# Attention half-steps reordered, and the change from experts to channel attention made half by half

## The chip, the cores and the metric

The kernel runs on one core of a Trainium2 chip. The metric is the device time of one execution in microseconds; lower is better. TensorE (PE) multiplies matrices and turns tiles, VectorE (DVE), ScalarE (ACT) and GpSimd (POOL) work on rows and elements, SyncE (SP) issues the transfers. Each has a queue of its own that runs in the order in which it was written, and they meet at semaphores.

## The reference

1,024 rows of 256 values (16 batches of 64 rows) go through four stages, each added to x behind a gain.

```
x = x + tanh(g_xattn[0]) * gated_attention(layernorm(x), ctx)    # 16 heads in 8 groups, own and cross, inputs rounded to fp8
x = x + tanh(g_ffn[0])   * experts(layernorm(x))                 # 32 experts, 8 chosen: silu(x wg) * (x wu) * share, then wd
x = x + tanh(g_xattn[1]) * channel_attention(layernorm(x), ctx)  # softmax over channels within each batch, 8 heads
x = x + tanh(g_ffn[1])   * mlp(layernorm(x))                     # four-bit weights: gelu(gate) * up, then down
```

## The kernel before, in words

**Gated attention** works in 16 units, two for each group: the first 512 rows, then the rest. Unit h has four tiles of 128 rows. Step h of the pipeline does the projections and norms of unit h, the scores and softmax of unit h-1 and the outputs of unit h-2. The order within a step is written by hand, once for each engine, in its `step(h)`. For tile i: TensorE's `project` puts queries, keys and values in PSUM; ScalarE's `squares` sums squares and `copy_values` takes the values; GpSimd's `rstd_of` makes the reciprocal deviation (an addition and a power); VectorE's `normalise` scales the rows; TensorE's `turn_tile` turns them; ScalarE's `keys` and VectorE's `queries` take the result. For half r of a unit: `scores`, VectorE's `shift` (maximum and difference), ScalarE's `exponent`, VectorE's `totals`, GpSimd's `normalise_probs`, TensorE's `turn_probs`, ScalarE's `probs_out`, TensorE's `values`, ScalarE's `take`, VectorE's `quantise` (five operations of rounding to fp8), TensorE's `outputs`, VectorE's `add_outputs`. `values(u, 0)` also waits for `add_outputs` of unit u-1.

The weights of the next group are prepared meanwhile. Even steps run `sum_weights` and `centre_weights` on w_in (halves c) and ScalarE's `weights_high`; odd steps run `weights_low` and `output_weights_low` (wp_lo). w_in and wp_in have one buffer each. SyncE issues w_in(g) once `weights_low` of group g-1 is done, then wp_in(g) once `output_weights_low` of group g-1 is done; so w_in(g+1) stands in the queue behind wp_in(g).

**Experts and the last stage** share `gated_mlp`: steps j and b, blocks of 128 hidden units, halves of 512 rows. A half block does two products (gate, up), then the previous one's `down` adds into four PSUM banks. At the end ScalarE copies these to outT, TensorE turns them into eight tiles, VectorE adds them to x in four updates. **Channel attention** then makes statistics, scaled rows h and their high and low parts (split); TensorE's `replicate` spreads them, `row_scores` go to VectorE's `maxima`, four pairs of heads a batch, and after `take_maxima` the loop over 16 batches begins. Ahead of the first product stand eight filler matmuls (`keep_busy`).

## Time and profile before

| what | us |
|---|---|
| median of 3 runs | 942.41 |
| lowest, highest | 941.45, 947.39 |
| the profiled execution's own time | 944.11 |
| its span in the trace | 942.30 |
| PE, DVE, ACT, POOL busy | 839.4, 707.2, 542.3, 320.5 |

The profiled execution is 1.8 us longer than its span, which leaves out what lies around the instructions, and 1.7 us above the median. Busy shares are means over stages with different limits. A line of a timeline has start and duration in us, engine, source line, operation, and what it writes and reads; a bracket tells how long the engine was idle before it and what ended that.

### The profile page before, as it was taken

The numbers are of one execution on the slowest core, as the hardware profiler recorded it, in microseconds if no ns is written. First come the engines' busy times: TensorE is split into PE (matmuls) and PEld (weight loads), VectorE is DVE, ScalarE is ACT, GpSimd is POOL, SyncE is SP. The second block draws the span as 40 slices with busy tenths as digits, with TensorE's granted clock in tenths as the row PEclk, the third lists the DMA queues.
The fourth block names the chain that finished last, engine by engine and source line by source line (L and its number), as shares of the span: only waits on it lengthen the run. The fifth ranks groups of instructions, "written<-read, shape, count | busy, mean of one in ns | idle before, by whom it ended". The sixth has DMA issues, their size and how long they took to land. (4 is left out here: it accounts for less than half of the span.)

```text
span 942.3 us, 16846 instructions
## 1 busy us (share of the span) xinstructions
PE 839.4 (89%) x6150; PEld 673.3 (71%) x6152; DVE 707.2 (75%) x1071; ACT 542.3 (58%) x1579; POOL 320.5 (34%) x458
## 2 busy tenths in 40 slices
PE   1678989998999899976999999998999997999997
PEld 1567788777877887864777888886555554888886
DVE  7787989999998998788575555555898986466643
ACT  5667778787877787752543333332577774333432
POOL 1233444444443444333333222210333544042420
PEclk9878999999999999979999999999999997999999
DMA  4101010101010100005323333220100002101001
GB/s 160 45 2 67 1 69 2 68 2 69 1 68 1 68 2 24 1 2 211 101 73 115 108 113 105 96 64 31 40 1 2 2 2 67 34 34 54 14 0 45
DMA packets 13705, 46.26 MB, mean 49 GB/s; under 512 B 1952, under 2 KB 5376, under 8 KB 11328
## 3 DMA queue, kind: packets, MB, share of 16 engines
q1 hardware_dynamic: 13488, 45.27, 14.0%
q8 instruction: 43, 0.70, 0.3%
q14 instruction: 30, 0.25, 0.1%
q10 hardware_dynamic: 144, 0.03, 0.0%
HBM read 44.12 MB, written 1.18 MB: 48 GB/s over the span
## 5 line engine op out<-in xcount | busy, mean ns | idle before, releaser
L418 ACT ACTIVATE square<-ps 128x128 bf16<-128x128 f32 x384 | 100.6, 287 | 31.6 <-PE ps L242 31.4
L242 PE MATMUL ps<-wt_hi,xq 128*128 128x512 f32 (+1 forms) x256 | 90.8, 371 | 11.4 <-DVE wt_lo L650 10.7
L1333 POOL TENSOR_TENSOR moe_w_lo<-moe_w_all,moe_w_hi 128x384 fp32r<-128x384 f32 x48 | 56.3, 1206 | 121.9 <-ACT moe_w_hi L1436 121.9
L575 POOL TENSOR_TENSOR rstd<-rstd,half_neg 128x6 f32<-128x6 f32 x64 | 94.5, 1476 | 5.0
L242 PE MATMUL ps<-wt_lo,xq 128*128 128x512 f32 (+1 forms) x256 | 85.7, 355 | 0.0
L580 POOL TENSOR_TENSOR probs<-probs,total 128x512 f32<-128x512 f32 x32 | 45.7, 1428 | 117.5 <-DVE total L696 117.5
L1788 ACT ACTIVATE ca_probs<-ps 128x512 f32<-128x512 f32 x128 | 69.5, 594 | 26.9 <-PE ps L1704 26.0
L1452 ACT CAST moe_in_hi<-moe_inner 128x512 fp32r<-128x512 f32 x48 | 29.8, 621 | 93.7 <-DVE moe_inner L1516 93.7
L418 ACT ACTIVATION_READ_ACCUMULATOR square<-ps 128x1 f32 x384 | 83.5, 218 | 0.0
L668 DVE TENSOR_TENSOR qn<-ps,rstd 128x768 f32<-128x768 f32 x64 | 60.4, 952 | 30.6 <-POOL rstd L575 30.4
L1370 PE MATMUL ps<-moe_hT_hi,moe_w_hi 128*128 128x512 f32 x192 | 75.7, 394 | 5.0 <-POOL moe_w_lo L1333 4.4
L1873 DVE TENSOR_REDUCE context_mx<-ps 128x4 f32<-128x1024 f32 x64 | 75.9, 1210 | 3.5 <-PE ps L1678 3.3
L251 PE MATMUL ps<-ident,qn 128*128 128x128 f32 x256 | 43.2, 294 | 38.1 <-DVE qn L668 37.7
L1370 PE MATMUL ps<-moe_hT_hi,moe_w_lo 128*128 128x512 f32 x192 | 75.4, 393 | 0.0
L1370 PE MATMUL ps<-moe_hT_lo,moe_w_hi 128*128 128x512 f32 x192 | 75.3, 392 | 0.0
L1506 DVE TENSOR_TENSOR moe_act_g<-moe_act_g,ps 128x512 f32<-128x512 f32 x48 | 33.0, 687 | 53.5 <-PE ps L1370 53.5
L242 PEld LDWEIGHTS ps<-wt_hi,xq 128*128 128x128 f32 x256 | 52.0, 203 | 20.7 <-DVE wt_lo L650 11.1
L1333 POOL TENSOR_TENSOR ffn_w_lo<-ffn_w_all,ffn_w_hi 128x384 fp32r<-128x384 f32 x28 | 34.5, 1263 | 84.8 <-ACT ffn_w_hi L1436 84.8
L571 POOL TENSOR_TENSOR rstd<-sumsq,eps 128x6 f32<-128x6 f32 x64 | 21.1, 330 | 119.3 <-ACT square L418 119.3
L251 PEld LDWEIGHTS ps<-ident,qn 128*128 128x128 f32 x256 | 28.7, 145 | 44.9 <-DVE qn L668 43.5
L315 PE MATMUL ps<-wp_hi,catq 128*128 128x256 f32 x240 | 59.3, 287 | 0.3 <-DVE catq L101 0.3
L315 PE MATMUL ps<-wp_lo,catq 128*128 128x256 f32 x240 | 58.9, 285 | 0.0
(229 smaller groups left out, 2432.5 us busy)
## 6 DMA issues: line engine op xcount, KB each, us to landing
moe_w_all<-in_experts SPq DMA_DIRECT2D x8, 1152.0 KB, 6.2
w_in<-in_wt SPq DMA_DIRECT2D x8, 1024.0 KB, 5.8
moe_shares<-route_rows SPq DMA_DIRECT2D x14, 384.0 KB, 3.7
wp_in<-in_wp SPq DMA_DIRECT2D x8, 512.0 KB, 3.5
moe_shares<-route_rows SPq DMA_DIRECT2D x14, 256.0 KB, 3.8
ffn_codes<-in_codes SPq DMA_DIRECT2D x8, 384.0 KB, 3.4
ffn_w_scales<-in_code_scales SPq DMA_DIRECT2D x8, 384.0 KB, 4.0
moe_shares<-route_rows SPq DMA_DIRECT2D x14, 128.0 KB, 3.1
```

Of the source, the lines that this page charges most:

```text
L242: last = mm(ps[:, first + bank, col:col + width], left[:, c, tokens], w[:, c, wcol:wcol + width], start=(j == 0), stop=(j == len(steps) - 1))
L251: last = nc.tensor.transpose(ps[:, bank, j * P:j * P + P], qn[:, i % 2, j, :], ident[:])
L315: last = mm(ps[:, out_bank(u) + j, q * HID:q * HID + HID], catq[:, f // HPG, f % HPG, t * P:t * P + P], w[:, f, :], start=(n == 0), stop=( ...
L418: last = nc.scalar.activation(square[:, i % 2, j, :], ps[:, bank, (j % 4) * P:(j % 4) * P + P], ACT.Square, scale=float(HD) ** -0.5, accum ...
L575: nc.gpsimd.tensor_tensor(rstd[:, i % 2, :], rstd[:, i % 2, :], k.half_neg[:, 0:6], ALU.pow).then_inc(s["rstd_ready"], 1)
L580: nc.gpsimd.tensor_tensor(probs[:, r], probs[:, r], total[:, r, :].unsqueeze(2).broadcast_to([P, 8, SEQ]), ALU.mult).then_inc(s["probs_rea ...
L668: nc.vector.tensor_tensor(qn[:, i % 2], both[:, 0:6], rstd[:, i % 2].unsqueeze(2).broadcast_to([P, 6, HD]), ALU.mult).then_inc(s["normed"], 1)
L1333: last = nc.gpsimd.tensor_tensor(w_lo[:, b, cols], w_all[:, b, cols], w_hi[:, b, cols].bitcast(F32), ALU.subtract)
L1370: last = mm(ps[:, bank, :], w[:, b, col:col + P], h[:, c, tokens], start=(n == 0), stop=(n == len(steps) - 1))
L1506: nc.vector.tensor_tensor(act_g[:, half, :], act_g[:, half, :], ps[:, U_BANK, :], ALU.mult).then_inc(s["gated"], 1)
L1788: nc.scalar.activation(probs[:, head, :], ps[:, B_BANK + n % 3, :], ACT.Exp, scale=float(C_DIM) ** -0.5).then_inc(s["b_taken"], 1)
L1873: nc.vector.tensor_reduce(dst, ps[:, bank:bank + 2, :].rearrange("p e (q l) -> p e q l", q=CH), AX.X, ALU.max).then_inc(s["a_taken"], 1)
```

## The change

In attention TensorE does the first projection, turns the probabilities of unit h-2, and does the value products ahead of turning tile 0; the value products of (h-1, 0) go ahead of turning tile 3. ScalarE follows that order. VectorE sums both halves of the next group's weights at the start of even steps, centres them ahead of the second shift, makes half of weights_low at the start of odd steps, and does the totals of (h-1, 1) ahead of the additions. In `gated_mlp` the last step's blocks run all of the first half, then all of the second; the first half is turned and added to x under the last blocks. From experts to channel attention the first half's statistics and rows are made there too; the second half is turned, added and scaled within channel attention, where the filler matmuls are gone. Changes of names, slots and counters that follow from that are left out; so is `turned_bank`, which puts the first half in banks 2 and 3.

```diff
@@ -349,15 +349,16 @@
                 here = is_unit(h)
                 if here:
                     project(h, 0)
-                    project(h, 1)
                 if is_unit(h - 2):
                     turn_probs(h - 2, 1)
+                if here:
+                    project(h, 1)
                 if is_unit(h - 1):
                     scores(h - 1, 0)
+                if is_unit(h - 2):
+                    values(h - 2, 1)
                 if here:
                     turn_tile(h, 0)
-                if is_unit(h - 2):
-                    values(h - 2, 1)
                 if is_unit(h - 1):
                     scores(h - 1, 1)
                 if here:
@@ -370,9 +371,10 @@
                     turn_probs(h - 1, 0)
                 if here:
                     turn_tile(h, 2)
-                    turn_tile(h, 3)
                 if is_unit(h - 1):
                     values(h - 1, 0)
+                if here:
+                    turn_tile(h, 3)
             pe.wait_ge(s["ident_in"], 16)
             for q in range(4):
@@ -466,21 +468,22 @@
                 g, here = h // 2, is_unit(h)
                 if here:
                     squares(h, 0)
-                    copy_values(h, 0)
-                    squares(h, 1)
                 if is_unit(h - 2):
                     probs_out(h - 2, 1)
                 if here:
+                    copy_values(h, 0)
+                    squares(h, 1)
                     copy_values(h, 1)
+                if is_unit(h - 2):
+                    take(h - 2, 1)
+                if here:
                     keys(h, 0)
                 if is_unit(h - 1):
                     exponent(h - 1, 0)
-                if is_unit(h - 2):
-                    take(h - 2, 1)
+                if here:
+                    keys(h, 1)
                 if h % 2 == 1 and g + 1 < GROUPS:
                     weights_high(g + 1, 1)
-                if here:
-                    keys(h, 1)
                 if h == 0:
                     scale_rows(3)
@@ -488,27 +491,28 @@
                     squares(h, 2)
                     copy_values(h, 2)
                     squares(h, 3)
+                if is_unit(h - 1):
+                    exponent(h - 1, 1)
+                if h % 2 == 0 and h > 0 and g + 1 < GROUPS:
+                    weights_high(g + 1, 0)
+                if here:
                     copy_values(h, 3)
                 if is_unit(h - 1):
-                    exponent(h - 1, 1)
+                    probs_out(h - 1, 0)
                 if h % 2 == 1 and g < GROUPS:
                     output_weights_high(g)
-                if h % 2 == 0 and h > 0 and g + 1 < GROUPS:
-                    weights_high(g + 1, 0)
-                if is_unit(h - 1):
-                    probs_out(h - 1, 0)
                 if here:
                     keys(h, 2)
+                if is_unit(h - 1):
+                    take(h - 1, 0)
+                if here:
                     keys(h, 3)
                 if h == 0:
                     weights_high(1, 0)
-                if h == 0:
                     act.wait_ge(s["c_in"], 16)
                     for c in range(CH):
                         nc.scalar.copy(ctx_hi[:, c, :], ctx_in[:, c, :]).then_inc(s["c_high"], 1)
-                if is_unit(h - 1):
-                    take(h - 1, 0)
             act.dma_start(vec[:], a["vec"]).then_inc(s["v_in"], 16)
@@ -754,6 +758,11 @@
             def step(h):
                 g, here = h // 2, is_unit(h)
                 ahead = g + 1 < GROUPS
+                if ahead and h % 2 == 0 and h > 0:
+                    sum_weights(g + 1, 0)
+                    sum_weights(g + 1, 1)
+                if ahead and h % 2 == 1:
+                    weights_low(g + 1, 0)
                 if here:
                     normalise(h, 0)
                 if is_unit(h - 1):
@@ -766,31 +775,30 @@
                 if h == 0:
                     quantise_rows(2)
+                    sum_weights(1, 0)
                 if is_unit(h - 2):
                     quantise(h - 2, 1)
                 if ahead and h % 2 == 0:
-                    sum_weights(g + 1, 0)
+                    centre_weights(g + 1, 0)
+                if ahead and h % 2 == 0 and h > 0:
+                    centre_weights(g + 1, 1)
                 if ahead and h % 2 == 1:
-                    weights_low(g + 1, 0)
                     weights_low(g + 1, 1)
                 if is_unit(h - 1):
                     shift(h - 1, 1)
-                if ahead and h % 2 == 0:
-                    centre_weights(g + 1, 0)
                 if here:
                     normalise(h, 2)
-                    normalise(h, 3)
+                if is_unit(h - 1) and h < LAST:
+                    totals(h - 1, 1)
                 if is_unit(h - 2):
                     add_outputs(h - 2, 0)
                     add_outputs(h - 2, 1)
                 if here:
+                    normalise(h, 3)
                     queries(h, 2)
-                if ahead and h % 2 == 0:
-                    sum_weights(g + 1, 1)
-                if is_unit(h - 1) and h < LAST:
-                    totals(h - 1, 1)
-                if ahead and h % 2 == 0:
-                    centre_weights(g + 1, 1)
+                if h == 0:
+                    sum_weights(1, 1)
+                    centre_weights(1, 1)
                 if h % 2 == 1 and h < LAST:
                     output_weights_low(g)
                 if h == 0:
...
+        HALF = TILES // 2
+        def blocks(j, b):
+            if isinstance(j, int) and (j, b) == (STEPS // 2 - 1, 1):
+                return [(blk, half) for half in range(2) for blk in range(NBLK)]
+            return [(blk, half) for blk in range(NBLK) for half in range(2)]
+        def at(j, b, p):
+            return 2 * NBLK * (2 * j + b) + p
+        def turns_first_half(j, b, p):
+            return isinstance(j, int) and (j, b, p) == (STEPS // 2 - 1, 1, NBLK + 1)
...
+        def share_slot(j, n):
+            return 2 if isinstance(j, int) and (j, n) == (STEPS // 2 - 1, 2 * NBLK - 1) else n % 2
...
             with pool.Fori(1, STEPS // 2) as j:
                 low(j, 0, True)
                 low(j, 1, True)
+            if moe:
+                k.channel.gpsimd_rstd(pool, 0)
...
+            def turn_out(half):
+                for o in range(CH):
+                    pe.wait_ge(s["out_copied"], CH * half + o + 1)
+                    for t in range(HALF * half, HALF * half + HALF):
+                        last = nc.tensor.transpose(ps[:, turned_bank(t // 2), (t % 2) * HID + o * P:(t % 2) * HID + o * P + P],
+                                                   outT[:, o, t * P:t * P + P], ident[:])
+                        if o == CH - 1 and t % 2:
+                            last.then_inc(s["turned"], 1)
...
+                    for p in range(2 * NBLK):
+                        half_block(j, b, p, first=first and (b, p) == (0, 0))
+                        if turns_first_half(j, b, p):
+                            turn_out(0)
+                        if p > 0:
+                            down(j, b, p - 1)
+                        elif b > 0:
+                            down(j, 0, 2 * NBLK - 1)
+                        elif not first:
+                            down(j - 1, 1, 2 * NBLK - 1)
             pe.wait_ge(turn.low, 2 * CH)
             if moe:
                 router.tensor_logits(pe)
             steps(0, True)
-            with pe.Fori(1, STEPS // 2) as j:
+            with pe.Fori(1, STEPS // 2 - 1) as j:
                 steps(j, False)
...
+            steps(STEPS // 2 - 1, False)
+            down(STEPS // 2 - 1, 1, 2 * NBLK - 1)
+            if not moe:
+                turn_out(1)
...
+            def out_copy(half):
+                act.wait_ge(s["d_done"], at(STEPS // 2 - 1, 1, NBLK * (half + 1)))
+                for o in range(CH):
+                    nc.scalar.copy(outT[:, o, half * 512:half * 512 + 512], ps[:, OUT + 2 * o + half, :]).then_inc(s["out_copied"], 1)
...
+                            if turns_first_half(j, b, n - 2 * NBLK * b):
+                                out_copy(0)
...
+            inner_high(STEPS // 2 - 1, 1, 2 * NBLK - 1, False)
+            if moe:
+                k.channel.scalar_high(act, 0)
+            out_copy(1)
         @block.vector
+            def update_rows(q):
+                dve.wait_ge(s["turned"], q + 1)
+                rows = x[:, 2 * q:2 * q + 2, :].rearrange("p t o -> p (t o)")
+                nc.vector.scalar_tensor_tensor(rows, ps[:, turned_bank(q), :], k.gain[:, gain:gain + 1], rows, ALU.mult, ALU.add
+                                               ).then_inc(s["x_updated"], 1)
...
+                if turns_first_half(j, b, p):
+                    update_rows(0)
+                if moe and last_step and p == NBLK + 2:
+                    k.channel.vector_means(dve)
                 dve.wait_ge(s["in_hi_done"], v + 1)
...
+                if turns_first_half(j, b, p):
+                    update_rows(1)
+                    if moe:
+                        k.channel.vector_stats(dve)
...
+            if moe:
+                k.channel.vector_rows(dve)
+            else:
+                for q in range(HALF // 2, TILES // 2):
+                    update_rows(q)
...
+    def vector_stats(self, dve):
+        for n in range(self.HALF):
+            dve.wait_ge(self.ends["x_updated"], n // 2 + 1)
+            self.nc.vector.bn_stats(self.stats[:, n, :], self.k.x[:, n, :]).then_inc(self.s["stats_done"], 1)
...
+    def vector_rows(self, dve):
+        row_scale(self.nc, dve, self.k.x, self.h, self.mv, self.rstd, self.s["rstd_step"], 0, self.s["row_normed"], (0,))
+        self.vector_low(dve, 0)
+    def scalar_high(self, act, t):
+        act.wait_ge(self.s["row_normed"], t + 1)
+        split_high(self.nc.scalar.copy, self.split, self.h, t, t + 1, self.s["h_high"])
...
+    def tensor_last(self, pe, banks):
+        for q, bank in enumerate(banks):
+            for o in range(CH):
+                pe.wait_ge(self.ends["out_copied"], CH + o + 1)
+                for t in range(2):
+                    tile = self.HALF + 2 * q + t
+                    last = self.nc.tensor.transpose(self.k.ps[:, bank, t * HID + o * P:t * HID + o * P + P],
+                                                    self.outT[:, o, tile * P:tile * P + P], self.k.ident[:])
+            last.then_inc(self.ends["turned"], 1)
+    def vector_last_update(self, dve, banks):
+        for q, bank in enumerate(banks):
+            dve.wait_ge(self.ends["turned"], self.HALF // 2 + q + 1)
+            rows = self.k.x[:, self.HALF + 2 * q:self.HALF + 2 * q + 2, :].rearrange("p t o -> p (t o)")
+            self.nc.vector.scalar_tensor_tensor(rows, self.k.ps[:, bank, :], self.k.gain[:, 2:3], rows, ALU.mult, ALU.add
+                                                ).then_inc(self.ends["x_updated"], 1)
...
+        LAST_BANKS = (OUT_BANK, B_BANK + 2)
...
-            keep_busy(nc, k, OUT_BANK, 8)
             pe.wait_ge(s["h_low"], 2)
             replicate(0, 0)
             replicate(0, 1)
+            k.channel.tensor_last(pe, LAST_BANKS)
             row_scores(0, 0)
+            pe.wait_ge(k.channel.ends["x_updated"], TILES // 2)
             replicate(1, 0)
             row_scores(0, 1)
             replicate(1, 1)
...
-            for t in range(FIRST_TILES):
-                act.wait_ge(s["row_normed"], t + 1)
-                split_high(nc.scalar.copy, split, h, t, t + 1, s["h_high"])
             for b in range(2):
                 for group in range(2):
                     take_rows(b, group)
+                    if (b, group) == (0, 0):
+                        for t in range(1, FIRST_TILES):
+                            k.channel.scalar_high(act, t)
...
                 pool.wait_ge(s["weighed"], i + 1)
-            row_rstd(nc, pool, mv, rstd, k.half_neg, s["stats_done"], 0, s["rstd_step"], 0)
+            def rest_high(first, last, n0):
+                pool.wait_ge(s["row_normed"], last)
+                for par in range(2):
+                    pool.wait_ge(*((s["values_set"], 2) if n0 + par == 0 else (s["rest_high"], n0 + par)))
+                    dst = split[0:64].rearrange("p (n b) f -> p n b f", b=2)[:, first:last, par]
+                    nc.gpsimd.tensor_copy(dst, h[64 * par:64 * par + 64, first:last]).then_inc(s["rest_high"], 1)
             pool.wait_ge(k.context.values_scaled, 1)
             values(0)
             values(1)
...
-            pool.wait_ge(s["rest_high"], 2)
+            k.channel.gpsimd_rstd(pool, 1)
+            rest_high(FIRST_TILES, TILES // 2, 0)
+            rest_high(TILES // 2, TILES, 2)
+            pool.wait_ge(s["rest_high"], 4)
             for b in range(2, BATCH):
                 values(b)
                 if b > 2 and b % 2 == 0:
...
-            row_stats(nc, dve, x, stats, mv, s["stats_done"], 0)
-            row_scale(nc, dve, x, h, mv, rstd, s["rstd_step"], 0, s["row_normed"])
-            for t in range(FIRST_TILES):
-                dve.wait_ge(s["h_high"], 2 * t + 2)
-                split_low(nc, split, h, t, t + 1, s["h_low"])
-            for pair in range(PAIRS):
-                maxima(0, pair)
+            k.channel.vector_last_update(dve, LAST_BANKS)
+            maxima(0, 0)
+            k.channel.vector_last_stats(dve)
+            maxima(0, 1)
+            for t in range(1, FIRST_TILES):
+                k.channel.vector_low(dve, t)
+            maxima(0, 2)
+            k.channel.vector_last_rows(dve)
+            maxima(0, 3)
             take_maxima(0)
             maxima(1, 0)
             for b in range(BATCH):
```

## Rows read from the trace of the kernel before

**Rows 1.** PE, PEld, DVE, ACT, POOL, clock, DMA of each pair of steps

```profile
76.40:126.63 50.23, 46.95 (x418) 39.97 (x417) 43.16 (x63) 38.17 (x152) 20.07 (x21) 0.97 0.09 33
126.63:173.07 46.44, 41.86 (x417) 37.61 (x416) 42.55 (x61) 35.86 (x146) 20.30 (x21) 0.96 0.09 35
173.07:221.16 48.09, 43.82 (x404) 37.47 (x403) 43.61 (x63) 36.68 (x148) 21.14 (x21) 1.00 0.09 34
221.16:266.61 45.45, 40.60 (x417) 36.27 (x416) 43.07 (x61) 36.09 (x146) 20.53 (x21) 1.00 0.10 36
266.61:315.45 48.84, 44.87 (x403) 38.78 (x403) 43.00 (x63) 36.55 (x148) 21.02 (x21) 0.97 0.09 34
315.45:360.91 45.46, 40.58 (x416) 36.27 (x416) 43.09 (x61) 36.08 (x146) 20.57 (x21) 1.00 0.10 36
```

**Rows 2.** Timeline of DVE at the start of an even step

```profile
219.96 1.17 DVE L656 TENSOR_TENSOR wp_lo<-wp_in,wp_hi 128x1024 fp32r<-128x1024 f32 x1
...
224.01 1.23 DVE L101 TENSOR_TENSOR catq<-scaled,power 128x1024 fp32r<-128x1024 bf16 x1
226.45 0.96 DVE L668 TENSOR_TENSOR qn<-ps,rstd 128x768 f32<-128x768 f32 x1 [1.21 <-POOL rstd L575]
```

**Rows 3.** Timeline of SP, the issue of w_in in that step

```profile
221.53 0.43 SPq L195 DMA_DIRECT2D w_in<-in_wt  x1
```

**Rows 4.** The tile w_in: its eight transfers, from issue to landing

```profile
DMA to landing us min/median/max: 5.0/5.8/6.9
```

**Rows 5.** Timeline of PE there: turning tile 0, then value products

```profile
227.46 0.66 PE L251 MATMUL ps<-ident,qn 128*128 128x128 f32 x4 [2.17 <-DVE qn L668]
...
228.26 1.16 PE L301 MATMUL ps<-pT,v_rows 64*128 64x128 f32 x16
```

**Rows 6.** Timeline of DVE, the rest of that step

```profile
231.12 0.43 DVE L97 TENSOR_SCALAR scaled<-scaled 128x1024 bf16<-128x1024 bf16 x1
...
235.09 0.94 DVE L633 TENSOR_REDUCE w_mean<-w_in 128x6 f32<-128x768 f32 x1
...
239.88 1.27 DVE L720 TENSOR_TENSOR acc<-acc,ps 128x512 f32<-128x512 f32 x2
...
244.30 1.27 DVE L97 TENSOR_SCALAR scaled<-scaled 128x1024 bf16<-128x1024 bf16 x1
...
248.43 0.96 DVE L668 TENSOR_TENSOR qn<-ps,rstd 128x768 f32<-128x768 f32 x1
```

**Rows 7.** Timeline of ACT, the take of (h-1, 0)

```profile
242.52 1.57 ACT L451 ACTIVATE scaled<-ps,r_smooth 128x256 bf16<-128x256 f32 x4 [0.18 <-PE ps L301]
```

**Rows 8.** Timeline of POOL, the probabilities of (h-1, 1)

```profile
243.64 1.65 POOL L580 TENSOR_TENSOR probs<-probs,total 128x512 f32<-128x512 f32 x1 [5.21 <-DVE total L696]
```

**Rows 9.** Groups of DVE by shape, 130 to 361 us: first quantising operation

```profile
L97 DVE TENSOR_SCALAR scaled<-scaled 128x1024 bf16<-128x1024 bf16 x19 | 14.1, 742 | 3.5 <-ACT scaled L451 3.5
```

**Rows 10.** Timeline of PE in step 14, its wait

```profile
367.48 0.65 PE L251 MATMUL ps<-ident,qn 128*128 128x128 f32 x4 [1.55 <-DVE qn L668]
```

**Rows 11.** Timeline of DVE in step 1, its wait

```profile
46.56 0.96 DVE L668 TENSOR_TENSOR qn<-ps,rstd 128x768 f32<-128x768 f32 x1 [2.00 <-POOL rstd L575]
```

**Rows 12.** Windows, columns as in rows 1 (the clock third from last)

```profile
135.00:140.00 5.00, 5.00 (x58) 4.54 (x57) 3.93 (x9) 2.80 (x6) 1.04 (x1) 0.79 0.00 0
...
652.70:665.40 12.70, 10.26 (x42) 5.42 (x40) 10.43 (x32) 3.77 (x8) 6.52 (x21) 1.00 0.35 125
...
785.00:790.00 5.00, 1.93 (x16) 0.58 (x16) 3.91 (x15) 2.43 (x3) 0.00 (x0) 0.56 0.00 0
```

**Rows 13.** Timeline of DVE from experts to channel attention

```profile
653.48 2.73 DVE L1554 SCALAR_TENSOR_TENSOR x_rows<-ps,gain,x_rows 128x512 f32<-128x512 f32 x4 [2.42 <-PE ps L1419]
...
665.44 4.62 DVE L1873 TENSOR_REDUCE context_mx<-ps 128x4 f32<-128x1024 f32 x4 [0.83 <-PE ps L1678]
...
671.02 1.23 DVE L1873 TENSOR_REDUCE context_mx<-ps 128x4 f32<-128x1024 f32 x1
```

**Rows 14.** Timeline of DVE at the end of the kernel

```profile
936.67 2.72 DVE L1554 SCALAR_TENSOR_TENSOR x_rows<-ps,gain,x_rows 128x512 f32<-128x512 f32 x4 [2.40 <-PE ps L1419]
```

142 lines of the change are left out of this document (70 added, 72 removed).

## The prediction

> **What bounds the kernel now.** I first read the split of the span into stages, one line for each pair of attention steps [rows 1]. Read the time of a pair beside its VectorE time. T stands here for the end of wp_lo, the low part of the output weights, which closes each pair of VectorE's queue. In the five pairs from 126.63 to 360.91 VectorE is busy 42.55 to 43.61 us of 45.45 to 48.84, TensorE 40.58 to 44.87. Neither is full: VectorE's idle time is 234.28 - 215.32 = 18.96 us in the five pairs, 3.8 us a pair. That is the most this reordering can win there.
>
> Then the order of time on VectorE. Behind T comes the quantising of (h-1, 0), to 225.24, and a wait of 1.21 us for the reciprocal deviation that GpSimd makes of ScalarE's squares; normalise(h, 0) starts at 226.45, T + 5.3 us [rows 2]. TensorE waits 2.17 us for that result, turns it, and only then does value products (1.16 us) [rows 5]. So both edits aim at real holes. At the change from experts to channel attention VectorE's four updates of x start at 653.48, the four maxima of the first batch at 665.44 and the next batch's first, from which on the loop runs, at 671.02 [rows 13]: there a serial chain bounds the time.
>
> **The sums half a step early.** In even steps sum_weights(g+1, 0) and (g+1, 1) now stand ahead of normalise(h, 0). They read w_in, which has one buffer. SyncE's queue has not changed: it issues w_in only behind wp_in, which waits for the same wp_lo. The issue is at 221.53, T + 0.4 [rows 3], and landing takes 5.8 us (5.0 to 6.9) [rows 4]: the weights are there at T + 6.2. VectorE would be free at 225.24, T + 4.1. Before, the first sum ran at 235.09, 14 us after T, and the transfer was hidden; now VectorE waits 2.1 us, makes both sums, 0.94 us each less overlap (1.75 us) [rows 6], and normalise(h, 0) starts near T + 7.9 instead of T + 5.3. Queued behind it are shift(h-1, 0), normalise(h, 1) and the quantising; TensorE's turn_tile(h, 0) waits for it, and ScalarE's keys for that. The 1.2 us wait for GpSimd disappears beneath the new wait.
>
> **Odd steps.** Half of weights_low (1.45 us, half of a block of about 3) goes to the head of the step, where it fills the wait for GpSimd. Some odd steps have such a wait, the one at 248.43 has none [rows 6]. This half of the edit costs nothing by itself.
>
> **Later in the step.** Before, the outputs' additions end at 241.1 [rows 6] and the take of (h-1, 0) at 244.1 [rows 7]: additions, value products, ScalarE's take form a chain of 3.0 us to the next quantising. VectorE covered it with a queries copy, a sum, totals and a centring; at 244.30 it starts without a wait. In the changed order the sum, the totals and the centring stand earlier, and only normalise(h, 3) and queries remain, 0.87 + 0.72 = 1.6 us. These two are the pitches of their rows, and the difference is a new wait of VectorE, 1.4 us in even steps. In odd steps wp_lo (1.17) [rows 2] still covers it but for 0.3. Totals earlier do help in another place: GpSimd's multiplication of probs, 1.65 us from 243.64 [rows 8], collides with the first quantising operation, which takes 1.27 us at 244.30 [rows 6]. The same operation has a mean of 742 ns over 19 calls, and a free one takes 0.43 [rows 6], so the excess is 0.31 x 19 = 6.0 us in five pairs [rows 9]. I credit 0.84 us a pair, that of the even step; behind the odd one stands the wait for w_in, which eats it.
> The Trainium skill, page Advanced Engine Details and Errata, section Mode Summary, says that VectorE's second port is shared with GpSimd, so that two-port operations and GpSimd's block each other. By that rule the quantising that no longer meets GpSimd is a free one each time. The trace agrees, with 1.27 us where GpSimd runs.
>
> **Value products ahead of transposes.** values(h-2, 1) moves into the hole before turn_tile(h, 0) at 1.1 us a step. In even steps that hole grows by more than 1.1, and scores(h-1, 1) waits for shift(h-1, 0), which is behind normalise anyway; so there it wins nothing. It wins where no weights are prepared: steps 14 and 15 where TensorE's wait is 1.55 us in step 14 [rows 10], and I take 1.1 off each, together -2.2 us. values(h-1, 0) ahead of turn_tile(h, 3) lets ScalarE take earlier: ScalarE then still owes keys(h, 3) before squares(h+1, 0), which leaves VectorE an odd-step wait of about 0.7 us.
>
> **Sum of attention.** A pair is VectorE's work, 43.06 - 0.84 = 42.2, plus idle 2.1 + 0.3 + 1.4 + 0.7, plus the small gaps that it has now, what is left of its 3.8 us of idle time without the marked waits, an estimate of 1.0 us: 47.7 with rounding. Five pairs 238.5 against 234.28: +4.2 us; the light pairs (45.45) lose 2.2 us each and the heavy ones (48.09, 48.84) win about 1 or less. The pair of 50.23 us (76.40 to 126.63) is long today, with VectorE idle for 7.1; with 47.7 and half a microsecond for its clock it is -1.8 or so. In step 1 weights_low fills a wait of 2.00 us at 46.56 [rows 11]: -1.3. **Clock:** between 135 and 140 us the granted clock is 0.79 [rows 12], so TensorE ran part of it at 1.2 GHz, behind a wait of an even step like that at 227.46. Two of the five pairs show a clock under 1.00 [rows 1]. The light pair with such a drop takes 46.44 and one without 45.45: 0.9 us for a drop. TensorE's wait before turn_tile is now about 3.1 us in each even step, so I expect four drops, +3.4 us (bounds: 0, and six at twice the price, 11). Attention: 4.2 - 1.8 - 1.3 - 2.2 + 3.4 = +2.3 us.
>
> **Experts to channel attention.** Half of the updates, stats, scalings and the first low split go into or behind the last expert blocks, where VectorE has waits. The eight early transposes cost TensorE some 0.9 us there, on the path, so its last product ends near 653.7 and the second half's first update, behind ScalarE's copy, the end of the block, the replicas and transposes, starts near 656.5 (an estimate; today's first update is at 653.48). From 652.70 to 665.40 VectorE is busy for 10.43 us [rows 12]; half of it is the second half's, 5.2, less 0.9 for a low split that goes ahead: 4.3. With four maxima of 4.62 us, and mT with its wait and the wait for row scores, 1.9 us between them, the next batch's first maximum comes at 656.5 + 4.3 + 4.6 + 1.9 = 667.3 against 671.02 [rows 13]: -3.7 us. The copy by GpSimd of the later tiles ends near 667, used only in the loop: hidden, and if it weren't, under 1 us. The filler matmuls (keep_busy) go, and TensorE has waits of 2 to 4 us among the first maxima. At the next change of stage it idled likewise and had 0.56 from 785 to 790 us [rows 12]. I charge 1.5 us (bounds 0 and 5). Net -2.2.
> The Trainium skill, page TensorE: Matmul & The Clock Gate, section on HAM oscillation, says that idle gaps throttle the engine again, so that work after each gap starts at half speed. It speaks against this removal and against the longer waits of the even steps; it is the second rival. No row shows this start without filler.
>
> **End of the kernel.** The first half is turned under the last products; the last block's low part is ready only after that, so its 0.9 us is hidden. At the end four updates from 936.67, 2.72 us to the end of the last [rows 14], become two, whose end is set by the turned second half; I take 0.5 us off for the two updates that no longer stand ahead. -0.5.
>
> **Sum:** +2.3 - 2.2 - 0.5 = -0.4 us on the profiled 944.11 (span 942.30): 943.7. The median of the runs is 942.41, 1.7 lower, so the forecast is **942.0 us**, no change that this kernel's measurement can tell (1% is 9.4 us).
>
> **Rivals.** *The port decides:* VectorE binds throughout, and 14 early quantisings get 0.6 us each, 8.4 instead of the 4.2 counted, no drop of the clock comes (-3.4) and none at the change of stage (-1.5): 942.0 - 9.1 = 932.9. For it speaks that VectorE is busy for 215.32 of 234.28 us in the pairs; against it that the new waits of 2.1 and 1.4 us are of fixed length. 0.16.
> *The clock decides, slower:* each wait before turn_tile (six even steps) costs 1.9 us instead of four at 0.9, and the channel stage starts with 10 us at 1.2 GHz, costing 5.1: 942.0 + 8.0 + 3.6 = 953.6. It crosses 951.8 when the six drops cost over 1.6 us each with the slow start. Against it: of five pairs with such waits two had a drop. 0.13.
> *The half-by-half change gives nothing back*, the loop of 16 batches being bound by something that starts no earlier (replicas, low split of the rest): 942.0 + 2.2 = 944.2. 0.13.
> *The wait for w_in does not appear*, because the rest of the step comes later anyway: five pairs at 45.6, that is 47.7 without the 2.1 of waiting: 942.0 - 10.5 = 931.5. Against it the two rows of issue and landing. 0.04. My forecast itself: 0.54.
>
> The likeliest and the third rival are no change; of the port rival and the last I put 0.14 beyond 1%, of the clock rival 0.10. The range of 932 to 953 reaches to both.
>
> **What would show it.** In the changed profile: VectorE's sum of weights waits about 2 us for a transfer of w_in in steps 2, 4, ... 12; normalise(h, 0) of even steps at T + 7.9; the first quantising operation at 0.43; light pairs near 47.7, heavy near the same; windows with a clock of 0.5 to 0.8 more often; the loop's first maximum of batch 1 some 12.5 us after the stage starts. If pairs are all near 45, I have the step's critical chain wrong.

## The result and the profile after

| what | before | after |
|---|---|---|
| median of 4 runs, us | 942.35 | 950.86 |
| lowest, highest | 941.45, 947.39 | 947.85, 952.5 |
| ratio, 95% interval | | 1.0074, 1.0038 to 1.0109 |
| profiled execution, its span | 944.11, 942.30 | 952.5, 950.7 |

The changed kernel is 8.5 us slower, and a ratio of 1 lies outside the interval. The time is inside my range, but the forecast was 942.0 us and no difference. The page of the changed kernel, its span, busy times and granted clock in 40 slices of 23.8 us:

```profile
span 950.7 us, 16789 instructions
...
PE 840.3 (88%) x6134; PEld 677.3 (71%) x6136; DVE 700.3 (74%) x1071; ACT 539.1 (57%) x1579; POOL 303.0 (32%) x460
...
PEclk9879989998999999989899999999599998999999
```

VectorE does 6.9 us less work than before (707.2) and the span is 8.4 us longer: what grew is idle time. The clock row has a 5 at slice 28 (counted from 0, 665 to 689 us), where channel attention begins. The pairs of attention steps, columns as in [rows 1]:

```profile
76.69:124.45 47.76, 44.78 (x407) 38.29 (x406) 42.22 (x63) 36.67 (x149) 17.99 (x20) 0.99 0.10 34
124.45:172.20 47.75, 42.48 (x418) 38.53 (x417) 41.86 (x61) 35.54 (x146) 18.44 (x20) 0.93 0.09 34
172.20:222.00 49.80, 44.66 (x402) 38.35 (x401) 42.31 (x63) 36.35 (x148) 17.91 (x20) 0.97 0.09 33
222.00:272.22 50.22, 41.92 (x418) 38.11 (x417) 41.86 (x61) 35.61 (x146) 18.92 (x20) 0.93 0.11 33
272.22:320.61 48.39, 45.00 (x402) 38.66 (x401) 42.44 (x63) 36.35 (x148) 17.59 (x20) 0.96 0.10 34
320.61:367.95 47.34, 41.24 (x418) 37.49 (x417) 41.77 (x61) 35.50 (x146) 18.91 (x20) 0.96 0.10 35
```

The last five take 243.50 us against 234.28, with VectorE busy 210.24 against 215.32, so idle 33.26 against 18.96. VectorE's waits in these five pairs (total, times, longest):

```profile
DVE w_mean L637 <- DMA w_in<-in_wt: 16.7, 5, 5.1
DVE scaled L97 <- ACT scaled L453: 8.8, 10, 1.7
DVE qn L672 <- POOL rstd L579: 3.3, 9, 0.6
```

16.7 + 8.8 + 3.3 = 28.8, and 4.5 of gaps make the 33.3. One even step, the one with the longest wait for w_in, on VectorE, with the issues of SyncE first and TensorE's first transpose last:

```profile
222.00 0.33 SPq L201 DMA_DIRECT2D wp_in<-in_wp  x1
222.38 1.64 SPq L195 DMA_DIRECT2D w_in<-in_wt  x1
```

```profile
230.69 1.81 DVE L637 TENSOR_REDUCE w_mean<-w_in 128x6 f32<-128x768 f32 x2 [5.13 <-DMA w_in<-in_wt]
232.42 0.95 DVE L672 TENSOR_TENSOR qn<-ps,rstd 128x768 f32<-128x768 f32 x1
...
250.18 0.43 DVE L97 TENSOR_SCALAR scaled<-scaled 128x1024 bf16<-128x1024 bf16 x1 [1.38 <-ACT scaled L453]
...
255.39 0.96 DVE L672 TENSOR_TENSOR qn<-ps,rstd 128x768 f32<-128x768 f32 x1 [0.61 <-POOL rstd L579]
```

```profile
233.42 1.11 PE L251 MATMUL ps<-ident,qn 128*128 128x128 f32 x4 [5.68 <-DVE qn L672]
```

The three waits of the forecast are there, in their places: for w_in, for ScalarE's take at the end, for GpSimd in the odd step. The first is the largest. The next stage begins 7.7 us later than before (the first line is of the kernel before):

```profile
431.31 0.33 SPq L1001 DMA_DIRECT2D route_r_rows<-in_router  x1
...
439.04 0.33 SPq L1009 DMA_DIRECT2D route_r_rows<-in_router  x1
```

From experts to channel attention, VectorE's timeline:

```profile
661.85 0.87 DVE L978 TENSOR_TENSOR rows_split<-rows_h,rows_split 64x256 fp32r<-64x256 f32 x2
664.46 1.41 DVE L1685 SCALAR_TENSOR_TENSOR x_rows<-ps,gain,x_rows 128x512 f32<-128x512 f32 x2 [1.74 <-PE ps L1677]
...
673.48 1.22 DVE L2009 TENSOR_REDUCE context_mx<-ps 128x4 f32<-128x1024 f32 x1
675.48 0.43 DVE L2015 CAST ca_mT<-ps 128x256 fp32r<-128x256 f32 x1 [0.78 <-PE ps L1816]
676.21 1.23 DVE L2009 TENSOR_REDUCE context_mx<-ps 128x4 f32<-128x1024 f32 x1 [0.30 <-PE ps L1808]
...
684.15 1.23 DVE L2009 TENSOR_REDUCE context_mx<-ps 128x4 f32<-128x1024 f32 x1 [2.95 <-PE ps L1808]
```

The second batch's first maximum is at 676.21 against 671.02 [rows 13]; attention being 7.7 us longer, the change of stage has won 2.5. Then the windows of the same stretch, clock third from last:

```profile
670.00:675.00 5.00, 2.15 (x10) 1.63 (x11) 4.61 (x8) 0.00 (x0) 2.61 (x4) 0.50 0.01 2
675.00:680.00 5.00, 5.00 (x27) 3.45 (x26) 2.91 (x4) 2.96 (x4) 0.76 (x1) 0.50 0.00 0
680.00:685.00 5.00, 5.00 (x26) 3.87 (x26) 2.05 (x2) 1.51 (x3) 0.00 (x0) 0.50 0.01 3
```

The granted clock is 1.2 GHz for 20.5 us (668.0 to 688.5), TensorE is busy all the time from 675 on, VectorE waits for it. From that maximum to the last stage's statistics the loop takes 113.81 us against 108.79. These statistics, before and after:

```profile
779.81 1.36 DVE L64 BATCH_NORM_STATS2 ffn_stats<-x_rows 128x6 f32<-128x256 f32 x4
...
790.02 1.36 DVE L64 BATCH_NORM_STATS2 ffn_stats<-x_rows 128x6 f32<-128x256 f32 x4
```

What follows is 0.9 us shorter at the end of channel attention and another 0.9 in the last stage. In all: attention +7.7, change of stage -2.5, loop +5.0, the ends -1.8, which is the 8.4 us.

This is the split of one pair of executions. The same attention orders as in the changed kernel end at 434.9 and 435.1 us in the traces of experiments 1 and 4 below, those of before at 428.2 and 429.6 in experiments 2 and 6: there the loss of attention is 5.3 to 6.9 us.

### The profile page after: what moved, and what is told of

Read it like the earlier page. It is cut to its first block and busy times, and to the rows that moved or that the text cites. A ratio compares the mean times of both kernels' runs of the same rounds, so it can differ in the third digit from the quotient of the medians.

```text
span 950.7 us, 16789 instructions
## 1 busy us (share of the span) xinstructions
PE 840.3 (88%) x6134; PEld 677.3 (71%) x6136; DVE 700.3 (74%) x1071; ACT 539.1 (57%) x1579; POOL 303.0 (32%) x460
## 5 line engine op out<-in xcount | busy, mean ns | idle before, releaser
L579 POOL TENSOR_TENSOR rstd<-rstd,half_neg 128x6 f32<-128x6 f32 x64 | 91.5, 1429 | 5.0
L242 PE MATMUL ps<-wt_lo,xq 128*128 128x512 f32 (+1 forms) x256 | 83.7, 348 | 0.0
L251 PE MATMUL ps<-ident,qn 128*128 128x128 f32 x256 | 47.5, 315 | 37.3 <-DVE qn L672 37.3
L672 DVE TENSOR_TENSOR qn<-ps,rstd 128x768 f32<-128x768 f32 x64 | 61.0, 952 | 15.0 <-POOL rstd L579 14.5
L251 PEld LDWEIGHTS ps<-ident,qn 128*128 128x128 f32 x256 | 31.6, 157 | 44.6 <-DVE qn L672 40.8
L453 ACT ACTIVATE scaled<-ps,r_smooth 128x256 bf16<-128x256 f32 x128 | 50.1, 474 | 17.7 <-PE ps L301 16.1
L584 POOL TENSOR_TENSOR probs<-probs,total 128x512 f32<-128x512 f32 x32 | 34.6, 1082 | 79.2 <-DVE total L700 79.1
```

Source lines behind the costliest of these rows:

```text
L242: last = mm(ps[:, first + bank, col:col + width], left[:, c, tokens], w[:, c, wcol:wcol + width], start=(j == 0), stop=(j == len(steps) - 1))
L251: last = nc.tensor.transpose(ps[:, bank, j * P:j * P + P], qn[:, i % 2, j, :], ident[:])
L453: last = nc.scalar.activation(dst[:, :, h, :], src[:, :, h, :], ACT.Copy, scale=r_smooth[:, kind, head:head + 1])
L579: nc.gpsimd.tensor_tensor(rstd[:, i % 2, :], rstd[:, i % 2, :], k.half_neg[:, 0:6], ALU.pow).then_inc(s["rstd_ready"], 1)
L672: nc.vector.tensor_tensor(qn[:, i % 2], both[:, 0:6], rstd[:, i % 2].unsqueeze(2).broadcast_to([P, 6, HD]), ALU.mult).then_inc(s["normed"], 1)
```

## The experiments

Each was timed beside the kernel before on its chip; ratios are to that, with their 95% intervals. The medians of the kernel before there were 943.3 to 945.9 us.

**1 and 2. Which part.** The kernel before with one part of the change each: the attention orders, or everything else.

> The attention part of the change alone, the rest as before. Theory A (two separate losses: the wait for w_in ahead of the sums in attention, the low clock after the filler was removed in the channel stage): about +7.5 us against the kernel before, 950, since attention ends 7.7 us later in the changed kernel and nothing later is touched. Rival B (all of the loss is attention's, the new transition is neutral): +8.5, 951. Rival C (the loss is the transition's): 942.

> The half-by-half change and the new end alone, attention as before. Theory A: the loop's first maximum comes about 2.5 us earlier than before, and some 20 us at 1.2 GHz behind it give back 4 to 5 us; the new end gives about 0.5: 943 to 944, +1. Rival B: 942.4, equal. Rival C: 950, +8. By the forecast's own sum without its clock charge it would be -4, 938.

951.56 us (ratio 1.006, 1.0033 to 1.0088) and 943.23 (0.9983, 0.9963 to 1.0004). The loss comes with the attention orders; the rest changes nothing that can be told. Together they make 1.0043, and with their intervals reach the 1.0074 of the whole.

The trace of experiment 1 (span 951.4 us) shows that not all of its loss lies within attention, though nothing else is changed: against the kernel before, attention is 3.6 us longer, the way from there to the second batch's first maximum 2.5, the loop 4.2 (112.97 us), the ends 1.2 shorter. The clock fell at the start of channel attention here too (0.50 from 661.3 to 664.5 and from 678.4 to 688.4 us), with the old change of stage and its eight fillers. In the traces of the kernel before and of experiment 6, with the same code there, it held. Whether the later start brought the fall in experiment 1, or chance, no run shows.

**3. w_in ahead of wp_in.**

```diff
             load_output_weights(0)
+            load_weights(1)
             for g in range(1, GROUPS):
-                load_weights(g)
+                if g + 1 < GROUPS:
+                    load_weights(g + 1)
                 load_output_weights(g)
```

> The changed kernel, with the transfer of w_in(g+1) issued ahead of wp_in(g), so that it waits only for weights_low and not for wp_lo. If the wait for w_in is what attention loses, the waits of 2.4 to 5.1 us ahead of the sums go (18.8 us in six steps), the pairs fall from 47.3 to 50.2 us to about 45.5, and the kernel to 950.9 - 12 = 939. If the pairs were bound by another chain (additions, value products, take) and the clock, it stays within 2 us of the changed kernel: 949 to 951.

933.45 us (0.9871, 0.9846 to 0.9895). SyncE issues w_in 6.9 us ahead of wp_in, no wait for w_in is left, and the pairs are

```profile
168.44:214.10 45.66, 43.67 (x402) 37.16 (x401) 42.23 (x63) 36.23 (x148) 18.07 (x20) 1.00 0.11 36
214.10:258.85 44.75, 40.20 (x418) 36.34 (x417) 41.67 (x61) 35.34 (x146) 19.31 (x20) 1.00 0.11 37
```

The five take 225.58 us, 17.9 fewer than the 243.50 with the wait of 16.7. So the wait was on the path in its full length, and all else that went with it, five stretches of lower clock among it, was worth 1.2 us. The median fell by 17.4 where I expected 12, more than the whole loss of 8.5. Experiment 4 shows the price of the clock alone: three of its pairs there (123.63, 218.68 and 316.42 us) had a clock of 1.00, 0.93 and 0.96, and take 47.25, 49.43 and 47.28 us; without their own waits for w_in (2.41, 4.59, 2.44) each is 44.84. The windows say why: around each of the falls VectorE is full, here in the changed kernel:

```profile
131.50:139.00 7.50, 5.74 (x47) 5.10 (x48) 7.33 (x12) 2.19 (x5) 1.13 (x1) 0.54 0.00 1
...
231.00:238.00 7.00, 4.58 (x45) 4.13 (x45) 6.90 (x11) 1.08 (x2) 0.81 (x1) 0.51 0.00 0
```

**4 and 5. Fillers at the change of stage**, in the changed kernel and in that of experiment 3. Small matmuls at the end of experts, ahead of TensorE's wait for x_updated and among the first maxima:

```diff
             if not moe:
                 turn_out(1)
+            else:
+                keep_busy(nc, k, G_BANK, 2)
...
+            keep_busy(nc, k, A_BANK + 3, 1)
...
-                spare(5)
+                spare(10 if pair == 2 else 24)
```

> The changed kernel with filler matmuls where TensorE waits around the start of the channel stage: two at the end of the experts, one ahead of the wait for the updates, 10 and 24 small ones instead of 5 and 5 behind row scores 2 and 3 of the first batch. If the half clock from 668 to 689 us is what the stage loses, the granted clock stays at 1.0 there and the kernel gets 4 to 6 us faster than the changed one: 945 to 947. If the clock there costs nothing (VectorE bound), 951.

> w_in issued early and the fillers at the start of the channel stage together. If the two losses are independent: 933.4 for the early transfer, minus the 4.1 us that the fillers gave alone: 929 to 930. If the clock's drop matters less when the kernel is shifted: 931 to 933.

946.72 us (1.0032, 1.001 to 1.0055) and 930.8 (0.986, 0.983 to 0.9889): 4.1 and 2.7 us fewer than without them, though in both cases the interval overlaps that of the kernel without fillers. In experiment 4 the clock is full in these windows,

```profile
670.00:675.00 5.00, 3.86 (x31) 2.83 (x31) 4.46 (x5) 2.50 (x4) 2.08 (x2) 1.00 0.02 3
675.00:680.00 5.00, 5.00 (x50) 3.49 (x49) 3.13 (x4) 3.11 (x6) 0.00 (x0) 1.00 0.00 0
```

and the loop takes 108.88 us, as before. In the profiled execution of experiment 5 the clock fell all the same for a part of the stretch (0.83 from 660 to 680 us), and the loop took 113.08: these fillers do not hold it each time.

Over all the traces, the loop's time follows the clock in the 10 us behind its first maximum. With the new change of stage and no filler (the changed kernel and experiments 2, 3 and 7 to 11) it was 0.50 in all eight, and the loop took 113.5 to 114.3 us. With fillers, new or old, the clock held in four (the kernel before, experiments 4, 6 and 12: 108.7 to 108.9 us) and fell in two (experiments 1 and 5: 113.0 and 113.1). The end of channel attention gives a part back: it takes 10.8 us in the four and 10.0 in the others. So the half clock costs some 4.1 us in all, an estimate, and as much as the fillers took off the median. Of the 12 runs of experiment 4 eight lie at 944.5 to 947.3 us and four at 949.1 to 950.6; that the clock fell in the four would fit, but no trace shows it.

**6. The early w_in on the kernel before**, the swap of experiment 3 alone.

> The kernel before, with only SyncE's order changed. There the sums stand 14 us behind the transfer's issue and never wait. So theory A expects 944 (within 1 us of the kernel before). If the early transfer helps by itself, by clearing the queues in another place, it would take some us off here too, and the gain of 17 us of the run with w_in early would not speak for the sums' wait.

942.11 us (0.9993, 0.997 to 1.0016), as expected. There the transfer was hidden; the swap is worth 17 us only beside the early sums.

**7. Sums late.** The changed kernel with both sums behind quantise(h-2, 1), just ahead of the centring.

```diff
-                if ahead and h % 2 == 0 and h > 0:
-                    sum_weights(g + 1, 0)
-                    sum_weights(g + 1, 1)
...
                     quantise(h - 2, 1)
+                if ahead and h % 2 == 0 and h > 0:
+                    sum_weights(g + 1, 0)
+                    sum_weights(g + 1, 1)
```

> The changed kernel with both sums moved from the head of the even step to just behind quantise(h-2, 1), nothing else. Theory A: no wait for w_in, T to normalise back to 5.3 us or less; but the sums no longer fill the wait for GpSimd's power, so the pairs are a little longer than with w_in early: 46 us, kernel 935 to 938. Rival (the new order of totals, additions and takes is the loss, 1.4 us waits in even steps): it stays above 945.

948.2 us (1.0045, 1.0028 to 1.0061): no wait for w_in, yet only 2.7 us won where I expected 13 or more; it is in the place that I had given the rival. VectorE's waits from 80 to 420 us, and their place:

```profile
DVE qn L672 <- POOL rstd L579: 20.1, 22, 2.5
DVE scaled L97 <- ACT scaled L453: 14.0, 13, 2.3
```

```profile
225.81 0.96 DVE L672 TENSOR_TENSOR qn<-ps,rstd 128x768 f32<-128x768 f32 x1 [1.49 <-POOL rstd L579]
...
234.36 1.81 DVE L637 TENSOR_REDUCE w_mean<-w_in 128x6 f32<-128x768 f32 x2
236.08 1.82 DVE L643 SCALAR_TENSOR_TENSOR w_in<-w_mean,w_in 128x768 f32<-128x768 f32 x2
```

At the head of the step the sums fill the wait for GpSimd. The five pairs take 12.8 us more than in experiment 3; of that VectorE's wait for GpSimd is 8.8 (12.3 against 3.5), that for ScalarE's take 2.6 (10.8 against 8.2), and a wait for ScalarE's copies of the values 1.2. The centring's 1.8 us had stood ahead of shift(h-1, 1) and normalise(h, 2) already, now the sums' 1.8 stand there too; I take that for the cause of the two smaller waits, which no run shows. The missing wait for w_in is the gain of experiment 3 over the changed kernel; that over the kernel before needs the sums at the head as well, and the data there.

**8 to 11. The order of TensorE and ScalarE.** I had priced "value products ahead" at nothing or a small gain. Experiment 8 is the changed kernel with VectorE's attention order of before. Experiment 11 is that with the late half of TensorE's and ScalarE's steps put back too, so that of these only the early half is changed. Experiments 9 and 10 stand on the kernel of experiment 3: with both orders of TensorE and ScalarE put back, and with the late half alone:

```diff
                     turn_tile(h, 2)
+                    turn_tile(h, 3)
                 if is_unit(h - 1):
                     values(h - 1, 0)
-                if here:
-                    turn_tile(h, 3)
```

> The changed kernel with VectorE's order of before: only TensorE's and ScalarE's orders in attention are changed, and the transition. Forecast's view (value products ahead win nothing where weights are prepared, 2.2 us in steps 14 and 15): against the run with the transition alone, 943.2, it is -2, 941. If value products ahead are worth their 1.1 us a step while VectorE has time, it is -8 and more, 935.

> The changed kernel with w_in(g+1) issued ahead of wp_in(g), and with TensorE's and ScalarE's attention order of the kernel before; VectorE's order is the changed one. Theory A (the whole gain of the early sums comes from VectorE's order, and the orders of TensorE and ScalarE add little once the sums are early): within 3 us of the 933.5 that the same kernel had with all three orders changed. Theory B (VectorE's order and the value products ahead need one another: the take must come earlier because less work of VectorE now covers it): 940 to 950, with VectorE's waits for ScalarE's scaled over 2 us in each step. Theory C (the value products ahead are a loss in any setting, as they were with VectorE's order of before): 920 to 928.

> The changed kernel with w_in early, and only the late half of the step put back on TensorE and ScalarE: tile 3 is turned ahead of the value products of (h-1, 0), and ScalarE's order from its squares of tile 2 on is that of before. If turning tile 3 behind the value products lengthens the chain additions, value products, transpose, keys, next squares here too: 925 to 931, below 933.5. If the early take is what VectorE now needs: 938 to 948, with the wait for scaled before the first quantising operation up from 1.4 to about 2.5 us or more. If it is only a loss beside VectorE's order of before: within 2 us of 933.5.

> The kernel with VectorE's order of before, of TensorE's and ScalarE's order only the early half changed: value products of (h-2, 1) ahead of turning tile 0, the late half as before. Beside 943.2 with neither half and 959.2 with both. If the late half (value products of (h-1, 0) ahead of turning tile 3) makes the loss: 941 to 945. If the early half makes it: 955 to 960. If each makes half of it: about 951.

| late half of TensorE, ScalarE | VectorE as before | VectorE changed, w_in early |
|---|---|---|
| as before | e11: 942.28 (0.9968, 0.9939 to 0.9998) | e10: 951.13 (1.0069, 1.0041 to 1.0097) |
| changed | e8: 959.18 (1.0161, 1.0135 to 1.0188) | e3: 933.45 (0.9871, 0.9846 to 0.9895) |

Experiment 9 gave 955.67 (1.0119, 1.009 to 1.0148), 4.5 more than 10: the early half is worth something beside the new order of VectorE, and nothing measurable beside the old (11 against 2). Experiments 8, 9 and 10 lie outside all that I had expected of them, on the slow side; only 11 came where expected.

The late half is worth 17 us in one direction with one order of VectorE and 18 in the other with the other. Each wrong pairing shows its wait. In experiment 8 TensorE's wait for VectorE's additions from 80 to 420 us (total, times, longest; 3.7 us in the kernel before), and one of them:

```profile
PE ps L301 <- DVE acc L724: 22.3, 14, 2.1
```

```profile
219.33 1.42 PE L301 MATMUL ps<-pT,v_rows 64*128 64x128 f32 x16 [1.56 <-DVE acc L724]
220.68 1.11 PE L251 MATMUL ps<-ident,qn 128*128 128x128 f32 x4
```

VectorE of before normalises tile 3 first and adds the outputs afterwards. Value products placed ahead of turning tile 3 wait for these additions, and the tile, long ready, waits behind them. In experiment 10 it is the reverse: VectorE adds first and normalises tile 3 after, TensorE wants tile 3 first, so value products and ScalarE's take come late:

```profile
218.96 0.66 PE L253 MATMUL ps<-ident,qn 128*128 128x128 f32 x4 [1.28 <-DVE qn L672]
...
219.76 0.94 PE L303 MATMUL ps<-pT,v_rows 64*128 64x128 f32 x12
```

```profile
222.62 0.43 DVE L97 TENSOR_SCALAR scaled<-scaled 128x1024 bf16<-128x1024 bf16 x1 [1.86 <-ACT scaled L454]
...
246.72 0.43 DVE L97 TENSOR_SCALAR scaled<-scaled 128x1024 bf16<-128x1024 bf16 x1 [3.00 <-ACT scaled L454]
```

The wait before the first quantising operation is 1.86 and 3.00 us where experiment 3 has 0.25 and 1.39; over the five pairs it is 24.3 us against 8.2.

**12. The second centring late**, on experiment 5:

```diff
-                if ahead and h % 2 == 0 and h > 0:
-                    centre_weights(g + 1, 1)
...
                     queries(h, 2)
...
+                if ahead and h % 2 == 0:
+                    centre_weights(g + 1, 1)
```

> The version with w_in early and the fillers (930.8), and in even steps the second centring stands behind queries(h, 2), where before it stood, so that 0.9 us of VectorE's work lies again between the additions and the first quantising operation, whose wait there was 1.4 us. If that wait is a real part of the pair, its cover is worth 0.9 us in each of six even steps: 925 to 927, and the wait for scaled at the even steps' ends 0.5 us. If the length of the pair is set by TensorE's and ScalarE's loop (additions, values, take) and VectorE's wait there is only slack: 930 to 932.

924.09 us (0.9787, 0.9758 to 0.9816). The wait at the even steps' ends is 0.62 instead of 1.39, and the pairs are 0.8 us shorter, five in 221.56 us against 225.59:

```profile
119.61:163.58 43.97, 40.21 (x418) 36.30 (x417) 41.65 (x61) 35.49 (x146) 19.29 (x20) 1.00 0.12 37
163.58:208.41 44.83, 43.63 (x402) 37.12 (x401) 42.21 (x63) 36.36 (x148) 18.06 (x20) 1.00 0.11 37
```

The wait of 1.4 us was no slack; work put into it came off the pair nearly whole. The first pair, in its clock, and the loop, which kept its clock here, differ too; six pairs at 0.8 us make some 5 of the 6.7 us between the medians the centring's, an estimate. This version is 2.1% faster than the kernel before (1.8 to 2.4%), and its median is 2.8% below the changed kernel's (924.09 against 950.86).

## Why the prediction was wrong, step by step

It forecast +2.3 for attention, -2.2 for the change of stage, -0.5 for the end; the profile has +7.7, +2.5 (-2.5 and +5.0) and -1.8. Four terms failed: the wait for w_in (10.5 us forecast, 16.7 measured), step 1 (-1.3, +0.3), steps 14 and 15 (-2.2, +0.7) and the half clock of channel attention (1.5, 5.0); the 3.4 us for the clock in attention, which did not come, hid a part of the first. One by one:

- **Five pairs**, 238.5 us plus 3.4 for the clock: measured 243.50 (240.9 and 240.1 in experiments 1 and 4), so 1.6 over. The parts: VectorE's work 210.2 (forecast 211.0); the waits for scaled 8.8 (8.5), for GpSimd 3.3 (3.5), the gaps 4.5 (5.0). All hold. The wait for w_in was 16.7 instead of 10.5, 6.2 us and the largest miss of a single term. In three of the steps it is 2.4 to 2.5: the weights land at T + 6.0 to 6.1 (forecast 6.2), but VectorE comes at T + 3.6 rather than T + 4.1. In two it is 4.13 and 5.13, for the transfer landed at T + 7.7 and T + 8.7; I had the maximum of 6.9 us in [rows 4] and took the median alone. In experiments 1 and 4 the five waits are 14.4 and 14.5 us, with one of over 4 us in each.
- **The clock in attention**: the drops came, five rather than four, but the 3.4 us did not, since VectorE was full meanwhile (experiment 3). I priced a drop from two pairs of [rows 1], and misread them: they differ by 0.99 us, which makes 4.0 for four drops. For the kernel before that price holds, since in experiments 2 and 6 too the light pairs with a clock of 0.96 take 46.5 us and those with 1.00 take 45.5; what failed is carrying it over to steps whose wait is VectorE's own.
- **The quantising operation** runs free at 0.43, and its mean over the 19 operations fell from 742 to 407 ns, 6.4 us. But GpSimd's multiplication still meets the second operation in half of them, 1.15 us at 237.45 beside GpSimd from 237.19 to 238.32; that operation takes 1.5 us more than before in the five pairs. VectorE's work fell by 5.1 us (215.32 to 210.24); I had credited 4.2.
- **First pair** -2.5 (forecast -1.8; my own sum, 48.2 against 50.23, gives -2.0).
- **Step 1**, -1.3: failed. Attention reaches the first pair 0.3 us later than before. The wait in [rows 11] is one of step 0 and not of step 1, and it is still there (first line). In step 1 weights_low now waits for ScalarE's high part, which I had not looked at:

```profile
45.78 0.96 DVE L672 TENSOR_TENSOR qn<-ps,rstd 128x768 f32<-128x768 f32 x1 [1.98 <-POOL rstd L579]
...
68.59 0.75 DVE L654 SCALAR_TENSOR_TENSOR wt_lo<-w_in,w_scale,wt_hi 128x512 fp32r<-128x512 f32 x1 [3.67 <-ACT wt_hi L399]
```

- **Steps 14 and 15**, -2.2: failed. TensorE's waits before turning tile 0 fell from 1.55 [rows 10] to 0.29 us, as forecast, but that was not the bound; and behind step 15 the first scores of the last unit come late:

```profile
414.89 0.69 DVE L687 TENSOR_REDUCE mx<-ps 128x8 f32<-128x512 f32 x1 [3.06 <-PE ps L271]
```

  Before, this wait is 1.09. In ScalarE's timeline the take (1.57 us) now stands ahead of the last queries and keys, and the scores begin 0.1 us behind these keys. The stretch from T of the last pair to the end of attention went up by 0.7 us instead of down by 2.2. No run tried step 1 or these two steps alone, so what their waits cost is argued.
- **Value products ahead cost nothing** (step of the same name): right by luck, only because VectorE's order was changed with it. By itself this edit costs 16 us (experiment 8 against 2). I costed each engine's reorder on its own, where they hang together at one place: the additions and tile 3.
- **Change of stage**: the second batch's first maximum 12.9 us after the stage begins (forecast 12.5), the win 2.5 instead of 3.7. **The half clock** was charged 1.5 us with bounds 0 and 5 and took the upper bound, 5.0 on the loop, of which 0.9 came back behind it. Experiment 4 shows it: the fillers bring the loop back to 108.88 us and the median down by 4.1. That the fillers held the clock in the kernel before is shown less well: it fell in one of the three traces that have them.
  The Trainium skill, page TensorE: Matmul & The Clock Gate, section on HAM oscillation, says that work behind idle gaps starts at half speed. The trace agrees: the clock fell at 668.0 us, behind waits of TensorE of 1.60, 1.42 and 0.64 us, and the work behind its wait of 2.85 us ran at 0.50, until 688.5. Such waits do not bring a fall each time: those of 1.58 and 1.91 us at this place in the kernel before brought none, and those of 1.58 and 1.92 in experiment 1 did.
- **The end**: -0.9 in the last stage where I had -0.5, and 0.9 at the end of channel attention, which I had not looked at and which came with the half clock of the loop in each trace (experiment 5).

Of the rivals, the clock rival's time (953.6) is nearest, and half of its mechanism is right: the slow start of channel attention, 5.0 us against its 5.1, if over 20.5 us and not 10. Its other half, drops of 1.9 us in each even step, is not: the drops cost nearly nothing, and the wait for w_in itself is what costs. The row that I put against "the wait does not appear" was right. Experiment 3 comes near that rival's time, 933.45 against 931.5, in part by luck: the wait was 16.7 and not 10.5, and it came off a longer kernel. The port rival wanted 8.4 us off VectorE's work, and 5.1 came; the half-by-half change did give its 2.5 us back.

## What to carry over

When a step of one engine is moved earlier, look up the transfer that feeds it in its queue: here one swap of two issues turned a loss of 0.7% into a gain of 1.3%. Orders of two engines that meet at two semaphores have to be changed together: price the pair of orders, never one of them, since the same edit was worth 17 us either way. A drop of the clock cost 4 us where TensorE is what the others wait for, and next to nothing in steps where VectorE is full behind its own wait; the same drop cost 1.0 us a pair in the kernel before. And one profiled execution is not the kernel: the same attention code ended 4 us apart in different traces.

## What the runs showed of the hardware

- Windows of 4.5 to 7.5 us with a mean granted clock of 0.51 to 0.66 came behind TensorE's long waits in even steps of the changed kernel (5.68 us at 233.42), and did not come in these five pairs of experiment 3, where such waits were under 1 us. At channel attention's start the clock stayed at 0.50 for 20.5 us although TensorE was busy throughout the last 13 of these.
- The same transfer of w_in landed 5.0 to 8.3 us after its issue. The slowest is the one whose issue took SyncE 1.64 us instead of 0.43.
- Rounding operations of VectorE (128x1024 bf16) took 0.43 us alone and 1.15 us beside GpSimd's multiplication of 1.13 us.
